# Moving the closing arithmetic of each batch one to two groups later in the first attention layer

## The reference

```python
q, k, v = Wq x + bq, Wk kv + bk, Wv kv + bv           # 16 heads of 16 channels, 512 positions
attn = softmax(where(kv_mask, scale * q^T k, -inf))   # per batch and head, 512 x 512
mean = attn v;  ex2 = attn (v * v)
std = sqrt(relu(ex2 - mean * mean))
xn = (x*m - mean_x) / sqrt(relu(var_x) + 1e-5) * m    # masked instance norm over the 512 positions
out = (xn * std + mean) * m
```

## Time and profile before

| | |
|---|---|
| Time, median of 3 runs | 1750.86 us (1742.66 to 1754.98) |
| Profiled execution, its own time | 1760.44 us |
| Its span | 1758.6 us, mean granted TensorE clock 0.968 |
| PE busy | 1644.4 us (94%) |
| DVE busy | 1261.0 us (72%) |
| ACT busy | 1061.1 us (60%) |
| POOL busy | 516.4 us (29%) |
| Chain that ended last | PE 57%, DVE 20%, ACT 7%, issue 6%, DMA 5%, SPq 3%, POOL 2% |

### The profile page before, as it was taken

How to read it: one execution, slowest core, us unless ns; L and a number is a source line. 1 busy time by engine, 2 the same in 40 slices (tenths; PEclk the granted TensorE clock), 3 DMA queues, 4 the chain that set the end, 5 groups by cost and what they waited for, 6 DMA issues and landing times.

```text
span 1758.6 us, 30853 instructions
## 1 busy us (share of the span) xinstructions
PE 1644.4 (94%) x10578; PEld 1133.5 (64%) x10578; DVE 1261.0 (72%) x2758; ACT 1061.1 (60%) x2351; POOL 516.4 (29%) x795
## 2 busy tenths in 40 slices
PE   6899989899898988999999999999999899999999
PEld 3333334343343345788878777888888788888888
DVE  2677878788787737998999889999999762323222
ACT  1465767667666657787877878788887741121111
POOL 0134555546445442332223222222232220000000
PEclk8799999999998998999999999999999899999999
DMA  4555355463543513233232534333333330000000
GB/s 155 162 172 170 104 154 142 143 187 107 148 130 117 160 49 86 66 78 76 66 95 74 144 81 116 91 92 92 92 90 81 97 114 1 25 0 25 0 25 13
DMA packets 112619, 167.97 MB, mean 96 GB/s; under 512 B 27464, under 2 KB 43208, under 8 KB 112336
## 3 DMA queue, kind: packets, MB, share of 16 engines
q1 hardware_dynamic: 88580, 132.15, 25.8%
q0 software_dynamic: 20992, 29.12, 6.8%
q10 hardware_dynamic: 2892, 4.72, 1.0%
HBM read 72.06 MB, written 34.60 MB: 61 GB/s over the span
## 4 chain that ended last, share of the span: by engine, by line
PE 57%; DVE 20%; ACT 7%; issue 6%; DMA 5%; SPq 3%; POOL 2%; ACTq 0%; DVEq 0%; POOLq 0%
PE ps L543 11%; PE ps L1951 9%; PE ps L1925 7%; PE ps L520 5%; DVE at_t L1403 4%; PE ps L1274 4%; DVE at_t L1408 4%; PE ps L1284 4%; PE ps L529 3%; PE ps L497 2%; PE ps L1223 2%; DMA rz<-shares 2%; PE ps L1930 2%; PE ps L1212 2%; ACT at_prob L1611 2%
## 5 line engine op out<-in xcount | busy, mean ns | idle before, releaser
L623 DVE TENSOR_REDUCE nmax<-ps 128x2 f32<-128x1024 f32 x256 | 310.5, 1221 | 139.2 <-PE ps L520 138.1
L788 ACT ACTIVATE prob<-ps 128x1024 f32<-128x1024 f32 x256 | 261.6, 1022 | 158.4 <-PE ps L529 154.1
L1611 ACT ACTIVATE at_prob<-at_t,at_nmax 128x256 f32<-128x256 f32 x512 | 256.6, 506 | 86.5 <-DVE at_nmax L1408 75.4
L543 PE MATMUL ps<-prob,v 128*64 128x512 f32 x1024 | 275.1, 630 | 0.2
L1408 DVE CUSTOM_DVE_ANT_0 at_t<-at_t,at_off 128x256 f32<-128x256 f32 x512 | 233.6, 493 | 8.8
L1769 POOL TENSOR_TENSOR at_low<-at_low,at_high 128x512 fp32r<-128x512 f32 x64 | 86.7, 1355 | 462.1 <-DVE at_high L1437 462.1
L2110 DVE CAST mlp_h_hi<-mlp_h 128x512 fp32r<-128x512 f32 x64 | 28.4, 444 | 212.9 <-ACT mlp_h L2022 179.9
L520 PEld LDWEIGHTS ps<-ring 64*128 64x128 f32 x512 | 49.5, 190 | 185.3 <-issue 133.9
L2022 ACT ACTIVATE mlp_h<-ps,b 128x512 f32<-128x512 f32 x48 | 33.1, 690 | 218.3 <-PE ps L1925 218.3
L1223 PE MATMUL ps<-ident,at_prob 128*128 128x128 f32 x1024 | 158.9, 278 | 0.0
L520 PE MATMUL ps<-ring 64*128 64x512 f32 x512 | 132.4, 514 | 22.3 <-DMA ring<-rows 10.0
(11 more groups left out here) (218 smaller groups left out, 3929.7 us busy)
## 6 DMA issues: line engine op xcount, KB each, us to landing
ring<-rows SPq DMA_DIRECT2D x62, 512.0 KB, 6.3
rows<-shares_of SPq DMA_DIRECT2D x90, 256.0 KB
at_k_stack<-at_high SPq DMA_DIRECT2D x256, 64.0 KB, 2.5
at_q_stack<-at_high SPq DMA_DIRECT2D x128, 64.0 KB, 2.7
at_q_stack<-at_high POOLq DMA_DIRECT2D x128, 64.0 KB, 2.4
at_q_stack<-at_low SPq DMA_DIRECT2D x128, 64.0 KB, 2.1
at_k_stack<-at_low POOLq DMA_DIRECT2D x128, 64.0 KB, 2.4
c_in<-in_ctx SPq DMA_DIRECT2D x8, 512.0 KB, 9.1
```

The source lines that it names most:

```text
L543: mm = eng.matmul(ps[2 * QD * k:2 * QD * (k + 1), VB, :], v[:, c, HG * G + 2 * p + k, :], prob[:, M % PROBS, k, :], start=(c == 0), stop=( ...
L623: eng.tensor_reduce(nmax[:, n % 2, j, 2 * p:2 * p + 2], ps[:, at:at + 2, :], AX, ALU.max, negate=True).then_inc(s_max, 1)
L788: eng.activation(prob[:, M % PROBS, :, :], ps[:, ST:ST + 2, :], ACT.Exp, scale=float(HD0) ** -0.5).then_inc(s_exp, 1)
L1611: ins = eng.activation(prob[:, m % 2, i, :], t[:, p, i, :], ACT.Exp, scale=-1.0, bias=nmax[:, m % 4, i:i + 1], accum_out=z[:, T % 2, j, 2 ...
```

## The change

The chain of a batch keeps its operations and their order, but nearly all of them move to a later group. `finish_shares` goes behind both regroups of group 4k+3, `mean_squared` to step 1 and `finish_variance` behind the first regroup of group 4k+4, the clip to step 5 of that group, `roots` to step 5 and `normal_x` to step 7 of the group after it, and `finish_x` (between the regroups) and `last_mask` (steps 6 and 7) to the group after that. The mask of a batch is thus needed longer, and there are four mask buffers. For the last chain before the end (batch 6) the steps in groups 32 and 33 are written out apart, and a small part of the second layer's statistics (`variances`) starts ten steps later. Lines of the changed kernel are numbered up to three higher.

```diff
-        mask = [None, sb("mask1", [P, D]), None]
+        mask = [None, None, None, sb("mask3", [P, D])]
...
-            eng.tensor_tensor(X[:, b, h, :], X[:, b, h, :], mask[b % 3][:], ALU.mult).then_inc(s_masked, 1)
+            eng.tensor_tensor(X[:, b, h, :], X[:, b, h, :], mask[b % 4][:], ALU.mult).then_inc(s_masked, 1)
...
-                if w % NG == 0 and 0 <= b - 2 < LAST and s == 2:
+                if w % NG == 0 and 0 <= b - 2 < LAST and s == (5 if w < GROUPS else 3):
                     positive_variance(b - 2)
-                if w % NG == 0 and 0 <= b - 2 < LAST and s == (6 if w < GROUPS else 5):
+                if w % NG == 1 and 0 <= b - 2 < LAST - 1 and s == 7 or (w, s) == (GROUPS, 6):
                     normal_x(b - 2)
-                if w % NG == 1 and 0 <= b - 2 < LAST and s in ((5, 6) if w < GROUPS else (2, 3)):
-                    last_mask(b - 2, (s + 1) % 3)
+                if w % NG == 2 and 0 <= b - 2 < LAST - 1 and s in (6, 7):
+                    last_mask(b - 2, s - 6)
+                if w == GROUPS + 1 and s in (4, 5):
+                    last_mask(b - 2, s - 4)
                 lead(w, s)
...
-            if b >= 3:
-                eng.wait_ge(s_masked, SB * (b - 2))
+            if b >= 4:
+                eng.wait_ge(s_masked, SB * (b - 3))
...
-                if s == 6 and w % NG == 3 and 0 <= b - 1 < LAST:
-                    mean_squared(b - 1)
-                if s == 3 and w % NG == 0 and 0 <= b - 2 < LAST:
+                if s == 1 and w % NG == 0 and 0 <= b - 2 < LAST:
+                    mean_squared(b - 2)
+                if s == 5 and w % NG == 1 and 0 <= b - 2 < LAST - 1 or (w, s) == (GROUPS, 4):
                     roots(b - 2)
                 lead(w, s)
...
             if n >= 0:
                 regroup(eng, 2 * n)
-            if w % NG == 3 and 0 <= b - 1 < LAST:
-                finish_shares(b - 1, 0)
-                finish_shares(b - 1, 1)
-            if n >= 0 and w % NG == 3:
-                regroup(eng, 2 * n + 1)
-            if w % NG == 3 and 0 <= b - 1 < LAST:
-                finish_variance(b - 1)
+            if w % NG == 0 and 0 <= b - 2:
+                finish_variance(b - 2)
             if w % NG == 0 and 0 < b < NB:
                 squares(2 * b)
             if w % NG == 2 and b < NB:
                 squares(2 * b + 1)
-            if n >= 0 and w % NG < 3:
-                regroup(eng, 2 * n + 1)
-            if w % NG == 0 and 0 <= b - 2:
+            if w % NG == 2 and 0 <= b - 2:
                 finish_x(b - 2, 0)
                 finish_x(b - 2, 1)
+            if n >= 0:
+                regroup(eng, 2 * n + 1)
+            if w % NG == 3 and 0 <= b - 1 < LAST:
+                finish_shares(b - 1, 0)
+                finish_shares(b - 1, 1)
+        finish_variance(LAST - 1)
         finish_x(LAST - 1, 0)
         finish_x(LAST - 1, 1)
...
-            if step == -47:
+            if step == -37:
                 variances(0)
-            if step in (-46, -41, -40):
-                inverse_roots(0, (-46, -41, -40).index(step) + 1)
+            if step in (-35, -34, -33):
+                inverse_roots(0, (-35, -34, -33).index(step) + 1)
```

More of the change, by code:

```diff
@@ L130, in layer0 @@
         rz = sb("rz", [P, SB, D])
-        mask = [None, sb("mask1", [P, D]), None]
+        mask = [None, None, None, sb("mask3", [P, D])]
         v_out = sb("v_out", [P, OUTS, D])
-        mask[0] = sb("mask0", [P, D])
+        mask[2] = sb("mask2", [P, D])
         with nc.sbuf_tensor("w_lo0", [P, SB, 3 * S], F32R) as w_lo0:
@@ L139, in layer0 @@
         far = sb("far", [P, D])
-        mask[2] = sb("mask2", [P, D])
+        mask[0] = sb("mask0", [P, D])
         ring = sb("ring", [P, RING, 4, D], F32R)
@@ L157, in layer0 @@
         loaded = sb("loaded", [P, 1])
+        mask[1] = sb("mask1", [P, D])
         x_hi, x_lo, c_hi, c_lo, w_hi0 = (g[name + "0"] for name in ("x_hi", "x_lo", "c_hi", "c_lo", "w_hi"))
@@ L652, in masked_x @@
                 made(eng, "q", 2 * b + 1)
-                eng.tensor_reduce(cnt[:, b, 0:1], mask[b % 3][:], AX, ALU.add)
-            eng.tensor_tensor_reduce(X[:, b, h, :], X[:, b, h, :], mask[b % 3][:], 1.0, 0.0, ALU.mult, ALU.add,
+                eng.tensor_reduce(cnt[:, b, 0:1], mask[b % 4][:], AX, ALU.add)
+            eng.tensor_tensor_reduce(X[:, b, h, :], X[:, b, h, :], mask[b % 4][:], 1.0, 0.0, ALU.mult, ALU.add,
                                      sums[:, b, 0, h:h + 1]).then_inc(links.sem, 1)
@@ L793, in masks @@
             eng.wait_ge(s_bits if b else s_first_bits, DMA)
-            if b >= 3:
-                eng.wait_ge(s_masked, SB * (b - 2))
-            eng.activation(mask[b % 3][:], m_in[:, b, :], ACT.Copy).then_inc(s_mask, 1)
+            if b >= 4:
+                eng.wait_ge(s_masked, SB * (b - 3))
+            eng.activation(mask[b % 4][:], m_in[:, b, :], ACT.Copy).then_inc(s_mask, 1)
             if b:
@@ L799, in masks @@
             eng.wait_ge(s_mask, b + 1)
-            eng.activation(far[:], mask[b % 3][:], ACT.Identity, bias=row[:, FAR_OFF:FAR_OFF + 1],
+            eng.activation(far[:], mask[b % 4][:], ACT.Identity, bias=row[:, FAR_OFF:FAR_OFF + 1],
                            scale=row[:, FAR_AT:FAR_AT + 1]).then_inc(s_far, 1)
```

## The result

The changed kernel is slower by 0.7%: a median of 1758.53 us (8 runs, 1751.46 to 1766.58) against 1746.70 us (8 runs) for the kernel before, a ratio of 1.0072 with a 95% interval from 1.0050 to 1.0094. That is 11.8 us more where 2.8 us less was forecast. The profiled execution has a span of 1762.8 us at a mean granted clock of 0.973.

The account below looks back on a forecast made before the run. TensorE was taken as the bound, losing 42.5 us in six groups 4k to stalls and low clock. Removing 42.5 and adding 36.9 gave -5.6 us, the layer's end +2.8: net -2.8, 1748 us, range 1733 to 1760.

Parts of the forecast that it names:

- Term 6: Groups 4k: finish_variance meets VectorE's small moments operations; +0.3 us per chain, +1.8 us, range 0 to 15.
- Rival B: GpSimd and VectorE get in each other's way in groups 4k: up to +18 us, 1764 us; chance 0.09.
- Terms 1 and 2: Start of groups 4k: ScalarE's wait for GpSimd's mean goes, -9.6 us; mean_squared at step 1 costs +5.1 us.
- Term 3: Roots move to step 5 of 4k+1: +15.3 us against 14.2 us removed, so the move gains nothing.
- Terms 4 and 5: Low clock kept behind the roots, +10.2 us, and at the start of groups 4k, +2.1 us, against 18.7 us removed.
- rivals A and C: Low clock goes with shorter stalls, 1736 us, chance 0.15; or low clock stays or doubles, 1765 us, chance 0.07.
- Rival C: Low clock follows every group start (+6.4) and doubles behind the roots (+10.2): 1765 us; chance 0.07.
- Term 7: Last masks in 4k+2 make VectorE some 2.6 us late at the start of 4k+3: +0.6 us, range 0 to 5.
- Term 8: Second regroup of 4k+3 leaves 8 us earlier, its DMAs beside the ring loads: +1.8 us, range 0 to 4.
- wait for ring rows: Start of groups 4k: TensorE's scores wait for ring rows; forecast to stay near 13 us after the change.
- Term 9: End of the layer: later roots cost +4.5 us, the mean's wait saves 1.75 us; net +2.75 us, range +1 to +5.
- Rival D: mean_squared waits for GpSimd's mean at its new place too, so that gain is lost: 1758 us; chance 0.03.

Follow-up runs that it names:

- e8: The changed kernel plus one GpSimd wait, for the end of VectorE's moments, before finish_variance; 1748.84 us, ratio 0.9995 to the kernel before.
- e10: e7 with the wait of e8 before finish_variance, and clip and roots one step later; 1742.09 us, ratio 0.9967 to the kernel before.
- e7: e6 with the roots and all behind them back in groups 4k and 4k+1; 1747.67 us, ratio 0.9994 to the kernel before.
- e6: The changed kernel with finish_shares back between the regroups and batch 6's chain back at its old places; 1745.71 us, ratio 0.9987 to the kernel before.
- e4: The kernel before with only roots, normal_x, finish_x and last_mask of batches 0 to 5 moved, and four masks; 1756.38 us, ratio 1.0045.
- e0: The kernel before, unchanged, run again for a second profile; 1744.67 us in one run, profiled span 1742.9 us.
- e5: The changed kernel plus a GpSimd wait for the group's last maxima before finish_shares; 1755.77 us, ratio 1.0045 to the kernel before.
- e2: The changed kernel with only finish_shares back in front of the second regroup of groups 4k+3; 1748.20 us, ratio 0.9997 to the kernel before.
- e3: The changed kernel with the value squares ahead of the first regroup in groups 4k; 1761.88 us, ratio 1.0067 to the kernel before.

## Why the prediction was wrong

The time lies in the range (1733 to 1760), but the change made the kernel slower where the forecast was slightly faster, and the step that failed is one term of the sum.

**Term 6, VectorE beside GpSimd in groups 4k: +1.8 us forecast, range 0 to 15.** This is the failed step. The scores' wait for maxima grew by 12.3 us, and e8, which keeps GpSimd's variance away from VectorE's moments and moves nothing else in the program, gives 10 us back. The 12.3 us lie within the range that I gave the term, but the sum took its near end. I had priced a hold of VectorE as the rest of one product (1.3 us), from rows in which it was so the earlier trace rows. I took the order of GpSimd's stream as harmless, since the engines meet no more often than before. The number of meetings was right, but not their length: the change put the products right behind DMA issues, four and three in a row. Rival B had the mechanism (GpSimd in VectorE's way in groups 4k), nearly the time (1764 us) and even the share of `finish_shares` at the group's start; it had a chance of 0.09 because the price per meeting was taken from before.

The Trainium skill, page "SBUF — State Buffer", section "Who interferes with whom", calls the shared ports an exclusive lock held for the whole instruction. The trace agrees where GpSimd had waited in front of its products; behind a DMA issue these runs show holds of three to five instructions in a row, up to 4.97 us, of which that sentence says nothing.

**Terms 1 and 2, the squared mean.** The wait went, as forecast. Its worth was read from the unlucky profile: there 8.7 us of the idle for exponentials were not the roots (20.9 less six times 2.03), in the second profile 6.0. At its new place it cost 0.43 us of idle per chain in e10, not 0.85. So this pair was worth some 3 us, not 4.5, and e7, which has it with the holds on the moments, shows 1.3 us of it in its idle sum and nothing in its time.

**Term 3, the roots.** TensorE idles 2.37 to 2.43 us at the new place, six times; the forecast was 2.4. That the move gains nothing was right, but the half to which it belongs costs 5 to 6 us of idle time, with the first half moved (e6 against e7) or not (e4 against e0). The times differ, 7 us and nothing, because the clock took 1 to 2 us in e4 and gave 4.5 us back in e6. What moves the clock so was not found.

**Terms 4 and 5, the clock.** The changed kernel's profile has less time at half clock in the groups (24.0 us for 37.4), but the mean granted clock of its 8 runs is 0.973, that of before's 31 runs is 0.973 too. What the sum put back for the clock, 12.3 us, is what the profile has (half of 24.0 us). What it took away, 18.7 us, was that of one execution: the second profile of before has 17.0 us at half clock, which cost 8.5. So the gain of 6.4 us was the difference between one execution and the usual one, and rivals A and C are both out. (Rival C also misread one row: the double stretch in group 28 follows the start of the group, not its roots.) Four low stretches behind the roots were forecast; the other three, behind the new idle times at the maxima, were not, and at 1.7 us each they belong to the price of term 6. Nor did the forecast think of the clock as something that such moves shift from one version to the next: against before on the same chip it is 0.0010 lower in e4 and 0.0038 higher in e6, which is a span of 8 us, more than most of the terms.

**Term 7, the last masks: +0.6 us forecast, range 0 to 5.** Turned scores waited 5.6 us in six places for the turned maxima's DMA, five of them in groups 4k+3 and one in group 17, for 0.9 and 2.2 us in the two profiles of before: 3 to 5 us, near the far end of the range. But the last masks aren't shown to be the cause: with the masks at the same place this row is 0.7 us in e8 and 7.7 us in e5.

**Term 8 and the ring rows.** I wrote that nothing would refute me sooner than the going of the wait for ring rows (13.2 us). It went: 2.9 us in one place. Yet the rows stayed the gate. In the profiles of both kernels the first scores of each of the six groups 4k start 0.1 to 0.25 us after the rows land, some 16 to 19 us after the first scores of the group before. But in five of the six groups TensorE now has work left until they land, since part of its idle time has gone to other places, such as the waits for the turned maxima in groups 4k+3. The sign was badly chosen: the row went and the gate stayed.

**Term 9, the end: +2.75 us forecast.** The idle times of e6 and e2 give 2.8 us. The idle was 8.71 us, where 9 to 10 were forecast.

**Rival D** did not occur: no wait of `mean_squared` is in the list. The books: 13.1 us more idle time than in the second profile of before and 2.8 us at the end make 15.9 us, and the mean clock is the same; measured were 11.8 us, with an interval from 9 to 16. They close to a few us and no better.

## What to carry to other kernels

When a step of one engine is moved, look at what now stands directly in front of it in that engine's own stream, and how long a run without a wait it joins; that, and not only the number of meetings, sets what the engine beside it pays. One wait that costs the waiting engine only time it has to spare (here GpSimd's, for the end of VectorE's moments) can be worth more than the move itself: with it the changed kernel is as fast as before, and half of the move with it is faster than both. Read each experiment twice, by the idle time of the engine that bounds and by the mean clock of all its runs: two kernels with the same idle time differed here by 0.5%. And predict from more than one profile where the clock varies: here two profiles of one kernel differ by 15.7 us, more than the change.

## What the runs showed of the hardware

GpSimd's elementwise products hold VectorE for whole runs. I counted in the thirteen profiles every VectorE operation of the first layer that was lengthened by over 0.3 us beside a run of four or five products. Where the run began right behind a DMA issue there were 17 such operations, all in the changed kernel, e3 and e8; each came while three to five products were still to end, and all 17 were held to the end of the run, 3.6 to 4.8 us beyond their own time. Where the run began behind a wait with idle time there were 157, and none was lengthened by more than 1.2 us, the length of one product.

Runs of two and three products are less clear: behind a DMA issue some operations waited for all of them, others were let in one product early; eleven square sums at the old variance were let in after the first of two. What in the instruction ahead of the run decides was not tried; e5, and one group of e8, show only that a wait with idle time in front of the run is enough; in its groups 4k e8 moves the run behind VectorE's work and so avoids the meeting.

The same kernel on the same chip ran from 1739.8 to 1759.4 us in 35 runs, and with 8 to 12 runs of the other kernel the intervals of the ratios are 0.13 to 0.27% wide to either side. Part of that spread is the clock of the single run, and the mean clock is a property of the version as well: 0.9774 for e6 and 0.9719 for e4, with 12 runs each.
